# The experts' short down chunk: high and low parts stacked on one set of partitions

## The reference

```python
E, TOP_K, H, I, SI = 8, 2, 256, 176, 704
shared = einsum('ts,sh->th', silu(x @ sw_gate) * (x @ sw_up), sw_down)
top_w, top_i = top_k(softmax(x @ router_w.T), TOP_K)   # weights then normed to 1
h = silu(einsum('th,ehi->eti', x, w_gate)) * einsum('th,ehi->eti', x, w_up)
expert_out = einsum('eti,eih->eth', h, w_down)
out = routed(expert_out, top_w) + sigmoid(x @ shared_gate_w)[:, None] * shared
```

## Time and profile before

| | us |
|---|---|
| median of 3 runs | 997.85 |
| lowest, highest | 994.13, 998.16 |
| the profiled execution | 999.12 |
| its span, first to last instruction | 997.1 |

### The profile page before, as it was taken

One profiled execution on the slowest core, in us unless ns is written; L12 is line 12 of the kernel. 1 busy time (PEld: TensorE's weight loads), 2 busy tenths in 40 slices (PEclk: granted clock), 3 DMA queues, 4 the chain that ended last, 5 costly groups with the idle time before them and its releaser, 6 DMA issues.

```text
span 997.1 us, 21097 instructions
## 1 busy us (share of the span) xinstructions
PE 882.9 (89%) x7200; PEld 719.8 (72%) x7200; DVE 704.8 (71%) x2130; ACT 693.2 (70%) x1538; POOL 260.6 (26%) x360
## 2 busy tenths in 40 slices
PE   4778899999899988888989898989888999899995
PEld 3556788888788975666666666666665888789884
DVE  6877788888855567778787778787777562365437
ACT  2878766867765358988888888888888322366646
POOL 0345622333432202002020102010100347334432
PEclk9989999999999989999999999999999999999997
DMA  6203022010000102011111111101020312244434
GB/s 191 65 1 107 5 72 86 12 33 23 22 23 23 43 12 65 2 26 42 26 40 27 38 30 33 34 10 46 9 62 23 101 55 94 70 112 113 113 129 183
DMA packets 54761, 54.87 MB, mean 55 GB/s; under 512 B 17953, under 2 KB 48929, under 8 KB 54658
## 3 DMA queue, kind: packets, MB, share of 16 engines
q1 hardware_dynamic: 51250, 44.18, 15.1%
q0 software_dynamic: 3408, 9.34, 2.8%
HBM read 32.85 MB, written 20.65 MB: 54 GB/s over the span
## 4 chain that ended last, share of the span: by engine, by line
PE 53%; DVE 18%; ACT 16%; issue 8%; DMA 2%; POOL 1%; another core or an unknown queue 1%; DVEq 0%; ACTq 0%; SPq 0%; POOLq 0%
PE ps L445 11%; PE ps L447 10%; PE ps L446 10%; PE ps L968 5%; PE ps L985 4%; ACT G L1487 4%; PE ps L676 3%; PE ps L956 3%; ACT wu_rows L1487 3%; ACT G L1497 2%; DVE G L2032 2%; PE ps L749 2%; PE ps L1154 1%; ACT RT L1247 1%; DVE wu_rows L2032 1%
## 5 line engine op out<-in xcount | busy, mean ns | idle before, releaser
L1487 ACT ACTIVATE G<-G,small 128x256 f32<-128x256 f32 x296 | 133.3, 511 | 25.2 <-DVE small L2032 25.0
L2032 DVE CUSTOM_DVE_ANT_0 G<-ps,nb 128x256 f32<-128x256 f32 x296 | 111.2, 420 | 44.1 <-PE ps L956 43.7
L445 PE MATMUL ps<-WU 128*128 128x256 f32 x384 | 117.0, 305 | 17.1 <-DVE wu_rows L1854 6.9
L1497 ACT COPY G<-ps 128x512 f32<-128x512 f32 x192 | 112.1, 584 | 13.9 <-PE ps L968 13.5
L2393 POOL TENSOR_SCALAR_AFFINE_SELECT G<-G 128x256 f32<-128x256 f32 x128 | 76.4, 620 | 146.5 <-ACT G L1332 146.3
L446 PE MATMUL ps<-WU 128*128 128x256 f32 x384 | 108.4, 282 | 0.0
L447 PE MATMUL ps<-WU 128*128 128x256 f32 x384 | 108.3, 282 | 0.0
L1487 ACT ACTIVATE wu_rows<-wu_rows,small 128x256 f32<-128x256 f32 x216 | 97.7, 510 | 15.2 <-DVE small L2032 14.9
L2032 DVE CUSTOM_DVE_ANT_0 wu_rows<-ps,nb 128x256 f32<-128x256 f32 x216 | 81.3, 420 | 32.4 <-PE ps L956 32.1
L968 PE MATMUL ps<-ident,G 128*128 128x128 f32 x592 | 91.8, 283 | 13.3 <-DVE G L2042 9.5
L2360 POOL TENSOR_SCALAR small<-small 128x2 f32<-128x2 f32 x16 | 7.0, 440 | 324.6 <-DVE small L1678 324.6
(11 more groups left out here) (251 smaller groups left out, 2374.4 us busy)
## 6 DMA issues: line engine op xcount, KB each, us to landing
xs<-G SPq DMA_DIRECT2D x8, 645.0 KB, 6.7
G<-xs SPq DMA_DIRECT2D x39, 128.0 KB
G<-x SPq DMA_DIRECT2D x17, 256.0 KB, 2.9
G<-in_x SPq DMA_DIRECT2D x16, 256.0 KB, 2.9
wu_rows<-yy SPq DMA_DIRECT2D x8, 512.0 KB, 6.9
x<-G SPq DMA_DIRECT2D x15, 256.0 KB, 2.2
wu_rows<-in_wu SPq DMA_DIRECT2D x8, 384.0 KB, 5.1
wraw<-in_wu SPq DMA_DIRECT2D x8, 256.0 KB, 3.0
```

What stands on the lines that cost most here:

```text
L445: pe.matmul(o, lh, rh, start=start, stop=False, skip_group_check=True)
L1487: m = act.activation(p, p, ACT.Exp, scale=-1.0, bias=mneg[:, k:k + 1])
L1497: act.copy(probT(h), halves(2 + h % 2)).then_inc(probT_act, 1)
L2032: m = dve.tensor_tensor_reduce(prob(H2 * i + h)[:, t, :], ps[:, SCORE_BANKS[h % 3], S * t:S * (t + 1)], nbv[:, t, :], 1.0, -FMIN, ALU.add, ...
```

## The change

The short chunk of a routed tile. DVE writes the 48 last hidden columns twice, in columns 128 to 175 and 192 to 239 of `hb`. After the transpose they lie on partitions 0 to 47 and 64 to 111. ACT takes the high part of all as before; DVE then replaces partitions 64 to 127 by the low part, in place. So one operand, `both`, holds the high part in its lower half and the low part in its upper half. The high down rows are loaded in both halves, and one pass of `both` against them adds high x high and low x high. A pass over the lower 64 partitions alone adds high x low. The last shared tile gets the same form with the halves changed over: the high hidden part stays in the upper half, the low one goes to the lower half, and the second pass works on partitions 64 to 127.

With that, `expert_down` loads the second chunk in a DMA of its own that reads 64 rows twice; the last shared tile's `product`, `hidden_hi` and `hidden_lo` work on 64 partitions; and POOL's zeros and their count in `consts3` are gone.

```diff
-        HG = [[cut(AF, 2560 + 512 * n + 256 * h, [2, P]) for h in range(2)] for n in range(2)]
+        HG = [(cut(AF, 2560 + 512 * n, [2, P]), AF[:, 2816 + 512 * n:2816 + 512 * n + P]) for n in range(2)]
...
+            if load == LOADS3 + 1 or (kind == 2 and e < NEXP - 1):
+                return 2
...
             def expert_down(e):
-                rows_e = bass.AP(wu3.tensor, UNIT * IE * e + 2 * KT * P, [[UNIT, P], [UNIT * P, 2], [1, E]])
-                sp.dma_start(wraw[:, 0:EX_DOWN].rearrange("p (c n) -> p c n", c=2), rows_e).then_inc(raw_ready, 16)
+                first = UNIT * IE * e + 2 * KT * P
+                sp.dma_start(wraw[:, 0:E], bass.AP(wu3.tensor, first, [[UNIT, P], [1, E]])).then_inc(raw_ready, 16)
+                twice = bass.AP(wu3.tensor, first + UNIT * P, [[0, 2], [UNIT, P // 2], [1, E]])
+                sp.dma_start(wraw[:, E:EX_DOWN], twice).then_inc(raw_ready, 16)
...
-                for to, of in ((slice(64, P), slice(0, 64)), (slice(0, 64), slice(64, P))):
-                    sp.dma_start(wraw[to, KT * P:HALF_UNIT], wu3[SH_FROM + SH_TILES - 1, of, 2 * KT * P:UNIT]).then_inc(raw_ready, 16)
+                for to in (slice(0, 64), slice(64, P)):
+                    sp.dma_start(wraw[to, KT * P:HALF_UNIT], wu3[SH_FROM + SH_TILES - 1, 0:64, 2 * KT * P:UNIT]).then_inc(raw_ready, 16)
...
                         tok = slice(P * t, P * (t + 1))
-                        m = product3(pe, ps[:, t // 2, E * (t % 2):E * (t % 2 + 1)], hh[:, tok], hl[:, tok],
-                                     shared(j, 0, at, E), shared(j, 1, at, E), j == 0 and t % 2 == 0, j == SH_TILES - 1)
+                        o = ps[:, t // 2, E * (t % 2):E * (t % 2 + 1)]
+                        if j < SH_TILES - 1:
+                            m = product3(pe, o, hh[:, tok], hl[:, tok], shared(j, 0, at, E), shared(j, 1, at, E),
+                                         j == 0 and t % 2 == 0, False)
+                        else:
+                            pe.matmul(o, hh[:, tok], shared(j, 0, at, E), start=False, stop=False, skip_group_check=True)
+                            m = pe.matmul(o, hh[64:P, tok], shared(j, 1, at, E)[64:P], start=False, stop=True, skip_group_check=True)
...
-                    for k in range(2):
-                        hi, lo = (WF[:, bass.ds(at + (EX * h + EX_GU + E * k), E)] for h in range(2))
-                        m = product3(pe, ps[:, i % 2, 0:E], HG[i % 2][0][:, k, :], HG[i % 2][1][:, k, :], hi, lo, k == 0, k == 1)
-                    m.then_inc(yo_done, 1)
+                    o, (h0, both) = ps[:, i % 2, 0:E], (HG[i % 2][0][:, k, :] for k in range(2))
+                    (hi, lo), (hi_twice, lo_one) = ([WF[0:rows, bass.ds(at + (EX * h + EX_GU + E * k), E)]
+                                                     for h, rows in ((0, P), (1, n))] for k, n in ((0, P), (1, 64)))
+                    product3(pe, o, h0, HG[i % 2][1], hi, lo, True, False)
+                    pe.matmul(o, both, hi_twice, start=False, stop=False, skip_group_check=True)
+                    pe.matmul(o, both[0:64], lo_one, start=False, stop=True, skip_group_check=True).then_inc(yo_done, 1)
...
-                    dve.tensor_tensor(hb[:, i % 2, 0:IE], ps[:, 2 + i % 2, IE:2 * IE], sgr[:, i % 2, :], ALU.mult).then_inc(h_ready, 1)
+                    bank = 2 + i % 2
+                    dve.tensor_tensor(hb[:, i % 2, 0:P], ps[:, bank, IE:IE + P], sgr[:, i % 2, 0:P], ALU.mult)
+                    rest = [P, 2, IE - P]
+                    dve.tensor_tensor(hb[:, i % 2, P:E].rearrange("p (c n) -> p c n", c=2)[:, :, 0:IE - P],
+                                      ps[:, bank, IE + P:2 * IE].unsqueeze(1).to_broadcast(rest),
+                                      sgr[:, i % 2, P:IE].unsqueeze(1).to_broadcast(rest), ALU.mult).then_inc(h_ready, 1)
...
-                    dve.tensor_tensor(HG[i % 2][1], ps[:, 4 + i % 2, 0:E].rearrange("p (k t) -> p k t", k=2),
-                                      HG[i % 2][0].bitcast(F32), ALU.subtract).then_inc(hg_ready, 1)
+                    dve.tensor_tensor(HG[i % 2][1], ps[:, 4 + i % 2, 0:P], HG[i % 2][0][:, 0, :].bitcast(F32), ALU.subtract)
+                    both = HG[i % 2][0][64:P, 1, :]
+                    dve.tensor_tensor(both, ps[64:P, 4 + i % 2, P:E], both.bitcast(F32), ALU.subtract).then_inc(hg_ready, 1)
...
-            pool.memset(sg_3[0:64, 2, :], 0.0).then_inc(consts3, 1)
```

More of the change, by code:

```diff
@@ L1117, in ranks @@
                 def ranks():
-                    pe.wait_ge(consts3, 16)
+                    pe.wait_ge(consts3, 15)
                     pe.wait_ge(mask_ready, 1)
@@ L1152, in h_turn @@
                         pe.wait_ge(hg_ready, i - 1)
-                    for k in range(2):
-                        m = pe.transpose(ps[:, 4 + i % 2, P * k:P * (k + 1)], hb[:, i % 2, P * k:P * (k + 1)], ident[:])
-                    m.then_inc(h_turned, 1)
+                    pe.transpose(ps[:, 4 + i % 2, 0:P], hb[:, i % 2, 0:P], ident[:])
+                    pe.transpose(ps[:, 4 + i % 2, P:2 * P], hb[:, i % 2, P:2 * P], ident[:]).then_inc(h_turned, 1)
                 def down_one(i):
@@ L1541, in hidden_hi @@
                         act.wait_ge(down_done[3], n - 1)
-                    act.copy(HT_3[n % 2][:, 0, :], hf_3[:, n % 2, :]).then_inc(hid_hi[3], 1)
+                    own = slice(0 if n % SH_TILES < SH_TILES - 1 else 64, P)
+                    act.copy(HT_3[n % 2][own, 0, :], hf_3[own, n % 2, :]).then_inc(hid_hi[3], 1)
                 def keep(b):
@@ L2122, in product @@
                     else:
-                        dve.wait_ge(consts3, 1)
-                        dve.tensor_tensor(hf_3[:, n % 2, :], ps[:, 2 + 2 * (n % 2), :], sg_3[:, 2, :], ALU.mult
+                        dve.tensor_tensor(hf_3[64:P, n % 2, :], ps[64:P, 2 + 2 * (n % 2), :], sg_3[64:P, 2, :], ALU.mult
                                           ).then_inc(prod_ready[3], 1)
@@ L2128, in hidden_lo @@
                     dve.wait_ge(hid_hi[3], n + 1)
-                    dve.tensor_tensor(HT_3[n % 2][:, 1, :], hf_3[:, n % 2, :], HT_3[n % 2][:, 0, :].bitcast(F32),
+                    last = n % SH_TILES == SH_TILES - 1
+                    own, lo = (slice(64, P), HT_3[n % 2][0:64, 0, :]) if last else (slice(0, P), HT_3[n % 2][:, 1, :])
+                    dve.tensor_tensor(lo, hf_3[own, n % 2, :], HT_3[n % 2][own, 0, :].bitcast(F32),
                                       ALU.subtract).then_inc(hid_ready[3], 1)
@@ L2144, in choose @@
                     dve.wait_ge(logits_done, BLOCKS3)
-                    dve.wait_ge(consts3, 16)
+                    dve.wait_ge(consts3, 15)
                     halves_of = ps[:, 7, 0:2 * GATES * TB].rearrange("p (b g) -> p b g", g=2 * GATES)
@@ L2461, in _ @@
             pool.memset(all_ones, 1.0).then_inc(consts3, 1)
-            pool.wait_ge(consts3, 10)
+            pool.wait_ge(consts3, 9)
             pool.memset(not_before, 0.0).then_inc(consts3, 1)
@@ L2469, in _ @@
             pool.iota(tile_no, [[1, SLOT_TILES + 1]], 0, 0, allow_small_or_imprecise_dtypes=True).then_inc(consts3, 1)
-            pool.wait_ge(consts3, 14)
+            pool.wait_ge(consts3, 13)
             pool.affine_select(out=not_before, in_=not_before, compare_op=ALU.is_gt, fill=-1.0, base=0, pattern=[[1, P]],
```

## The result

The changed kernel takes 1002.61 us (median of 6 runs, 1001.33 to 1006.38) against 997.25 for the kernel before (6 runs, 994.13 to 998.16): a ratio of 1.0063, 95% interval 1.0043 to 1.0083. It is slower by 5.4 us. The profiled execution took 1002.96 us, its span is 1000.9, and the mean granted clock 0.969.

The account below looks back on a forecast made before the run. The prediction took a 2.31 us routed-tile loop through POOL's store and the register load to hide PE's own 2.11. Terms 3.6 + 1.1 + 0.5 - 0.8 = +4.4 us took the median 997.85 to 1002.3, range 995.0 to 1008.5.

Parts of the forecast that it names:

- A change of height: On PE, each switch between 64-row and 128-row passes costs 0.20 us: 0.09 late start plus 0.11 uncovered weight load.
- the signs: Checks in the new trace: a routed tile's last down pass lasts 0.39 us and starts 0.2 after its neighbour.
- Which bound holds: Routed tile: the loop through POOL's store and the register load binds before (2.31 us), PE's own work after (2.39 to 2.42).
- The first rival: The 0.20 us wait ahead of a routed tile's transposes stays, the register load being late for its own reason: 1010 us, chance 0.12.
- The routed term: Routed tiles: 0.09 us more for each of 37 tiles, 3.3, plus 0.28 and 0.08 for the last two: +3.6 us.
- The tail: Last shared tile's final block, before DVE's closing chain: its longer down passes delay the end by +0.5 us.
- The weights' two DMAs: expert_down's DMAs: POOL's split may start a DMA's issue time later, but POOL idles before its first scatter: 0.
- Blocks 0 and 1: Last shared tile: their longer passes are absorbed, at no cost; a rival had up to 2.2 us show, about 1005.3, chance 0.13.
- the clock: PE's granted clock, 0.91 from 852.3 to 871.7 us before, was counted in the sum as a gain of 0.8 us.
- block 2: Last shared tile: its down passes take 2.5 us instead of 1.4, +1.1 us of PE's work.
- DVE: Routed tiles: split products and low parts add at most 0.37 us a tile, covered by idle time: nothing; rival 1006, chance 0.03.
- The cheap pass: Rival: a 64-row pass costs what a full one does, or no switch is paid: 995.0 us, chance 0.14.

Follow-up runs that it names:

- addresses-ahead: Kernel before, with all 39 register loads of the experts' addresses moved from the routed loop to the shared stage: 989.32 us, ratio 0.9920.
- no-stores: Kernel before, with POOL's scattered store left out for 36 of the 39 routed tiles: 991.10 us, ratio 0.9944.
- the shared half alone: Kernel before, with only the last shared tile changed and the routed tiles as before: 996.42 us, ratio 1.0000.
- the change with addresses ahead: Kernel changed, with all 39 register loads of the experts' addresses moved from the routed loop to the shared stage: 1002.38 us, ratio 1.0057.
- the routed half alone: Kernel before, with only the routed tiles changed and the last shared tile as before: 1004.64 us, ratio 1.0071.
- full rows: Kernel changed, with its 64-row passes made 128-row passes, which adds low x low to the sum: 998.55 us, ratio 1.0006.
- the grouped kernel: Kernel changed, with the last shared tile's four full passes first and its four 64-row passes after them: 1001.35 us, ratio 1.0044.
- filled: The routed half alone, with 18 unread passes put on PE ahead of the first gathered tile's transposes: 999.98 us, ratio 1.0035.

## Why the prediction was right, and where its terms were off

The forecast of 1002.3 against 1002.61 holds, and so does its mechanism. The closeness of the two is luck: the base was taken as 997.85 where it is 997.25, the step as +4.4 where it is +5.4, and one term was left out. The terms are less exact than their sum.

- **A change of height, 0.20 us.** 0.19 in the routed tile, by the starts (0.38 for two) and by the runs with and without it (0.37). The 64-row pass lasts 0.38 and starts 0.20 after its neighbour, as the signs asked. The row for it came from another stage with the same widths; that was enough.
- **Which bound holds.** The store and the register load held the kernel before (the addresses-ahead and no-stores runs each free it, to 2.11 and 2.17), PE's own work holds the kernel changed (addresses ahead gives it nothing). The wait ahead of the transposes went from 7.1 to 0.2 us. The first rival falls: neither the wait nor 1010 came. The prediction's tie of the load to the store was right, though POOL's instruction is already over when the load starts.
- **The routed term, +3.6** (its parts, 3.3, 0.28 and 0.08, make 3.7). Measured +3.2. The period after is 2.373 where 2.39 to 2.42 was forecast, against 2.30 before (2.31 in the twenty tiles that the prediction took): 0.07 a tile in place of 0.09, +2.4 in place of +3.3. The last tiles, where 0.36 was forecast, gave 0.8. The two errors nearly cancel.
- **The tail, +0.5.** Measured +0.6 in this pair. But the shared half alone and the change with addresses ahead both have 33.5 us there against 33.4 before. A term of this size is not shown.
- **The weights' two DMAs, nothing.** This term was put at nothing because POOL idles 4.55 us ahead of its first scatter. The wait for the down rows grew by 3.2 us, POOL's idle time fell to 1.91, and the split came to run beside DVE's slot arithmetic, whose last stretch then took 0.6 to 0.7 us longer. In the profiled change PE does not wait for the first gathered tile, so no late tile shows there; whether PE's 0.57 us at 852.91 come of DVE's delay is open. Where PE does wait for it (the routed half alone, full rows, the grouped kernel), a later scatter can reach the time; no run prices it apart.
- **Blocks 0 and 1, nothing; the clock, -0.8; block 2, +1.1.** Together they were to give +0.3. Measured to the first store: 0.0 in the pair, and a ratio of 1.0000 for the shared half alone. In the pair the parts can be read: PE starts behind its wait 0.57 later, block 2's passes take 1.1 more, and the fall of the clock, 1.7, did not come. But the split into three terms is worth less than their sum, since other kernels' traces have the waits and the falls elsewhere: the first gathered tile bounds the entry of the routed stage as well, and I had not looked at it. In the profiled change PE does not wait for that tile; in the grouped kernel, earlier by its shorter down passes, it waits 3.00 us.
- **DVE, nothing.** The two products and two low parts are as long as the estimate (0.29 + 0.25, 0.28 + 0.29), and DVE idles 27 us ahead of them.
- **The cheap pass, rival of the other side.** Full rows is that rival made real: 998.55, ratio 1.0006, where it had 995.0. Its loop (2.25) is right, and its gain was overrated: the loop of the kernel before had been 2.30, so that a tile gave 0.02 and not 0.06, and the wait of 4.91 us and the clock at the entry were not in it.

One thing argued for the sum stays unproven: the pair of traces gives +3.8, the medians +5.4. The clock fall at 853 us is present in the one execution profiled before, and I can't say how many of its other runs had it. Four more traces have the shared tile as before (the routed half alone and filled, the kernel before with addresses ahead and without stores), and none has a fall at 853 us; they are of other kernels, so they only point the same way. If the runs mostly had none, the -0.8 should have been 0, and the sum +5.2.

## What to carry over

Before passes are saved by working on fewer rows, look at what their neighbours' height is: here one short pass alone among full ones cost two changes, 0.37 us, where the pass that it did away with took 0.12. If it can take the full height, with terms that do no harm, do that; if not, put the short ones together. And ask which bound hides the saving: here the shorter PE work alone gives nothing (1.0006), the addresses ahead 0.9920, and both together 0.9891, because PE's saving was hidden under the store and the register load. And look at what a change adds beside the engine that it is for: the second DMA of the down rows took POOL's idle time from 4.55 to 1.91 us and slowed DVE.

## What was not expected of the hardware

- Idle time of PE has a second price. After waits of 4.41 and 4.91 us the granted clock was 0.67 and 0.59 in the next 7 and 6 us; 18 passes whose results nobody reads, put into such a wait, took the ratio from 1.0071 to 1.0035.
- A load of one value into a register of TensorE's queue, 0.30 us by itself, took up to 0.68 when it started 1.30 to 1.60 us after the start of GpSimd's scattered store, whose instruction lasts 0.96, and bound a loop of 2.3 us through it.
- A busy share of 100% (81.07 of 81.07 us in the routed stretch) hides what PE pays for changes of height: 0.38 us in each tile are late starts and weight loads that no pass covers.
- Two DMAs of 128 KB in place of one of 256 KB made POOL wait 6.07 us instead of 2.83 for the last expert's down rows. While POOL split them, one instruction of DVE took 0.70 us instead of 0.17.
